# Mamba and mixture-of-experts block on one core: row sums by accumulating DMA, f16 dt projection, a folded prologue, a new instruction order, and the residual added by TensorE

## The reference

```python
h = layernorm(x) * (1 + ca) + sa
x = x + ga * mamba(h)          # mamba(h) = out_proj(y) + h
h = layernorm(x) * (1 + cb) + sb
x = x + gb * moe(h)

# mamba: xi, z = split(rmsnorm(h) @ in_proj); xi = silu(causal conv of 4 taps (xi))
#   dt (16), B (16), C (16) = split(xi @ x_proj);  delta = softplus(dt @ dt_proj + b)
#   state (512 channels x 16): s = s * exp(delta * A) + delta * B * xi, along the sequence
#   y = (sum over the 16 states of s * C) + xi * D;  y = y * silu(z)
# moe: 16 experts and a shared one (two more in the kernel's layout); sigmoid gate, the 4 largest
#   of 16 normed as weights; silu(x @ win) * (x @ vin) * weight, @ wout, summed
```

## Time and profile before

| | |
|---|---|
| time, median of 3 runs | 3053.87 us (3050.2 to 3055.23) |
| profiled execution | 3054.61 us, span of its records 3052.8 us |
| TensorE matmuls busy | 2488.1 us (82%), 16524 instructions |
| VectorE busy | 2568.1 us (84%), 3986 |
| ScalarE busy | 1830.3 us (60%), 3484 |
| GpSimd busy | 2563.1 us (84%), 2379 |
| DMA | 187.97 MB, mean 62 GB/s |

### The profile page before, as it was taken

The page is one execution under the profiler, slowest core; times in us unless marked ns, Lnnn a source line. Parts: engine busy times, 40 slices in busy tenths (PEclk is TensorE's granted clock), DMA queues, the critical chain, the costliest instruction groups (busy, mean ns, idle before and its releaser), DMA issues.

```text
span 3052.8 us, 52878 instructions
## 1 busy us (share of the span) xinstructions
PE 2488.1 (82%) x16524; PEld 1983.2 (65%) x16524; DVE 2568.1 (84%) x3986; ACT 1830.3 (60%) x3484; POOL 2563.1 (84%) x2379
## 2 busy tenths in 40 slices
PE   2566988879888797988879798887979888797979
PEld 0344766757676675767667576776757667576767
DVE  3579899888898988889898888889888898988953
ACT  2666666666666665665657566665656656665531
POOL 1689898989989898998989889898988989898942
PEclk7557998999999998999989899999989999999989
DMA  1311111211112111121112111121212211111101
GB/s 64 107 56 58 64 56 64 71 57 61 56 61 72 62 61 53 60 68 64 63 52 77 56 60 59 64 66 55 74 41 73 68 56 60 60 58 58 67 32 49
DMA packets 62150, 187.97 MB, mean 62 GB/s; under 512 B 12040, under 2 KB 14728, under 8 KB 61488
## 3 DMA queue, kind: packets, MB, share of 16 engines
q1 hardware_dynamic: 61872, 184.58, 18.0%
HBM read 166.68 MB, written 17.87 MB: 60 GB/s over the span
## 4 chain that ended last, share of the span: by engine, by line
POOL 29%; PE 27%; DVE 17%; issue 16%; ACT 9%; DVEq 1%; POOLq 1%; ACTq 0%; DMA 0%
POOL db_sb L639 12%; PE bank_ps L1236 9%; DVE states L995 7%; POOL y_sb L651 6%; PE moe_ps L1251 6%; PE rows_ps L1178 5%; POOL act L681 3%; POOL y_sb L659 2%; PE bank_ps L1160 2%; ACT da_ps L839 2%; DVE y_sb L1014 2%; DVE bank_ps L950 2%; DVE act L1089 1%; PE bank_ps L1134 1%; POOL du_sb L628 1%
## 5 line engine op out<-in xcount | busy, mean ns | idle before, releaser
L639 POOL TENSOR_TENSOR db_sb<-du_sb,b_sb 128x512 f32<-128x512 f32 x1024 | 1296.6, 1275 | 0.1
L1178 PE MATMUL rows_ps<-ident,states 128*128 128x128 f32 x4096 | 673.2, 295 | 163.7 <-DVE states L995 94.3
L651 POOL TENSOR_TENSOR y_sb<-y_sb,c_rows 128x512 f32<-128x512 f32 x512 | 655.1, 1280 | 169.8 <-ACT c_rows L817 169.8
L839 ACT ACTIVATE da_ps<-delta,a_sb 128x512 f32<-128x512 f32 x1024 | 701.8, 687 | 85.7 <-DVE states L995 84.2
L1178 PEld LDWEIGHTS rows_ps<-ident,states 128*128 128x128 f32 x4096 | 535.3, 153 | 281.9 <-DVE states L995 133.0
L1251 PE MATMUL moe_ps<-eout_sb,act 128*128 128x256 f32 x2304 | 627.7, 396 | 85.2 <-POOL act L681 83.5
L1236 PE MATMUL bank_ps<-h2T_high,ein_w_high 128*128 128x256 f16 x2304 | 644.0, 280 | 21.8 <-DVE delta L971 12.0
L995 DVE TENSOR_TENSOR_SCAN states<-da_ps,carry,db_sb 128x512 f32<-128x512 f32 x512 | 648.4, 1274 | 15.0 <-ACT da_ps L839 13.2
L1236 PE MATMUL bank_ps<-h2T_high,ein_w_low 128*128 128x256 f16 x2304 | 643.1, 279 | 0.0
L1236 PE MATMUL bank_ps<-h2T_low,ein_w_high 128*128 128x256 f16 x2304 | 642.4, 279 | 0.0
L995 DVE TENSOR_TENSOR_SCAN states<-da_ps,db_sb 128x512 f32<-128x512 f32 x512 | 616.2, 1213 | 23.2 <-ACT da_ps L839 13.0
(11 more groups left out here) (156 smaller groups left out, 2851.1 us busy)
## 6 DMA issues: line engine op xcount, KB each, us to landing
b_sb<-b_dram SPq DMA_DIRECT2D x128, 512.0 KB, 3.6
w_sb<-w_dram SPq DMA_DIRECT2D x128, 512.0 KB, 4.0
th_p<-x_dram SPq DMA_DIRECT2D x16, 512.0 KB, 5.8
r_dram<-conv SPq DMA_DIRECT2D x16, 512.0 KB, 2.6
x<-r_dram SPq DMA_DIRECT2D x16, 512.0 KB, 3.8
out_dram<-x SPq DMA_DIRECT2D x32, 256.0 KB, 2.2
mod_p<-mod_dram SPq DMA_DIRECT2D x8, 384.0 KB, 6.2
x<-e_in_dram SPq DMA_DIRECT2D x5, 512.0 KB, 4.6
```

The source lines that it names most:

```text
L639: pool.tensor_tensor(db_sb[:, n % NDB, :], du_sb[:, slots[t][0][0], b, :], b_sb[:, k % NBPAIR, s % BPAIR, :], ALU.mult).then_inc(sem["scal ...
L651: pool.tensor_tensor(place, place, c_rows[:, n % NCR, :], ALU.add).then_inc(sem["c_added"], 1)
L839: ac.activation(da_ps[n % NDA][:, :], delta[:, slots[t][0][0], b, :], ACT.Exp, scale=a_sb[:, b, s:s + 1]).then_inc(sem["exp_done"], 1)
L1178: last = pe.transpose(rows_ps[j % 2][:, b * P:b * P + P], states[:, step % 2 * NB + b, j * P:j * P + P], ident[:, :])
```

## The change

* **Rows.** ScalarE scales all four row blocks (`c_scale`), two at a time into one buffer of `c_rows`. `gather` is gone, and `c_add` is no GpSimd addition but a DMA that GpSimd issues for each pair of row blocks and that adds 128 x 1024 numbers into `y_sb`; the next step's DMA of the same pair waits for its landing.
* **Residual.** `r_gate`, `r_add`, `r_store` are gone. h itself is stored (`h_store`) and loaded again in the mix stage (`h_load`, into a new buffer `h_mix`); TensorE adds it in the out projection's bank, by a matmul with the identity, and `r_load` fetches x. The gate row leaves `mod_p`.
* **dt.** `xd` is computed transposed, four f32 matmuls of 512 columns that give 48 rows. ScalarE (`dt_high`) and VectorE (`dt_low`) split dt into f16 halves stacked on 80 partitions (`dt16`), against weights stacked likewise, so that `dtp` is four f16 matmuls. `xd_evac` is now ScalarE's and makes the rows directly; four transposes give C back as columns (`xd_t_evac`, VectorE).
* **Buffers.** `NDB` 6 to 5, `WROWS` 4 to 1: one expert's weights for each load, two buffers of one.
* **Prologue.** The blocks before slot 0 are gone. Their steps stand in the common order before and within slot 0 and wait only for what they need; x is the fourth load; the first sequence's modulation rows are computed first, with the condition vector repeated in 128 columns, and copied from PSUM (`mod0_rows`). No semaphores are cleared.
* **Order.** All places in the order are set anew: constants, `SHIFT` by name, and new tables `PLACE` (by name and index), `FIRST`, `LAST` and `START`.

```diff
-NDA, NDB, NCR = 2, 6, 3
-C_ACT = (1, 3)
-C_DVE = tuple(j for j in range(NJ) if j not in C_ACT)
+NDA, NDB, NCR = 2, 5, 3
+CPAIR = 2
...
-WROWS, NWROWS = 4, 2
+WROWS, NWROWS = 1, 2
...
-LEAD_P0, LEAD_P, LEAD_M = 2.059, 8.0, 1.42
...
-SLOT = 67.197
...
+LEAD_P0, LEAD_P, LEAD_M = 6.1001, 7.9891, 2.1125
...
+SLOT = 70.6876
...
+                    def first_loads():
+                        sp.dma_start(ct_sb, c_t).then_inc(sem["ct_in"], 16)
+                        sp.dma_start(wmod_sb[:, :, 0:2 * DM], w_mod[:, :, 0:2 * DM]).then_inc(sem["wmod_in0"], 16)
+                        sp.dma_start(norm_sb[:, :], norm_w).then_inc(sem["in_w_in"], 16)
+                        x_load(0)
+                        sp.dma_start(in_raw, in_w).then_inc(sem["in_w_in"], 16)
...
-                    def r_store(t):
-                        sp.wait_ge(sem["r_made"], nP(t) + 1)
...
+                    def h_store(t):
+                        for half in range(2):
+                            sp.wait_ge(*h_done(t, half))
+                        sp.dma_start(h_dram[bass.ds(slots[t][1][1], 1)].rearrange("o p n -> (o p) n"),
+                                     h_sb.rearrange("p j n -> p (j n)")).then_inc(sem["h_out"], 16)
...
+                    def h_load(t):
+
+                        sp.wait_ge(sem["h_out"], 16 * nP(t - 1))
+                        if nM(t):
+                            sp.wait_ge(*bank_full(("op", last_mix(t), NJ - 1)))
...
-                    def c_add(t, s, j):
+                    def c_add(t, s, pair):
...
+                        if step:
+                            pool.wait_ge(*c_adds(n - NJ // CPAIR))
...
-                        pool.tensor_tensor(place, place, c_rows[:, n % NCR, :], ALU.add).then_inc(sem["c_added"], 1)
+                        pool.dma_start(y_sb[:, slots[t][0][0], CPAIR * pair:CPAIR * pair + CPAIR, :], c_rows[:, n % NCR, :, :],
+                                       accum_op=ALU.add).then_inc(c_adds(n)[0], 16)
...
                         ac.wait_ge(sem["h_rms_done"], nP(t) + 1)
-                        ac.wait_ge(sem["r_gated"], nP(t) + 1)
+                        ac.wait_ge(sem["h_out"], 16 * (nP(t) + 1))
...
+                        for at in (DT_HIGH, DT_AGAIN):
+                            ac.activation(dt16[at:at + RANK, :], bank(("xd", t))[0:RANK, :], ACT.Copy).then_inc(sem["dt_high_done"], 1)
...
+                        ac.activation(c_rows[:, n % NCR, j % CPAIR, :], rows_ps[j % 2][:, :], ACT.Copy,
+                                      scale=xd_sb[:, slots[t][0][0], j, s:s + 1]).then_inc(sem["c_scaled"], 1)
...
-                        for j in range(NJ):
-                            for b in range(NB):
-                                last = pe.matmul(bank(key)[:, j * XD:j * XD + XD], u_sb[:, b, j * P:j * P + P], xproj_sb[:, b, :],
-                                                 start=(b == 0), stop=(b == NB - 1))
+                        for b in range(NB):
+                            last = pe.matmul(bank(key)[0:XD, :], xproj_sb[:, b, :], u_sb[:, b, :], start=(b == 0), stop=(b == NB - 1))
...
-                        pe.matmul(bank(key), dtw_sb[:, b * P:b * P + P], xdT[0:RANK, :], start=True, stop=True).then_inc(bank_full(key)[0], 1)
+                        pe.matmul(bank(key), dtw16[:, b * P:b * P + P], dt16[:, :], start=True, stop=True).then_inc(bank_full(key)[0], 1)
...
-                            pe.wait_ge(*(c_scales(*before) if before[1] in C_ACT else gathers(*before)))
+                            pe.wait_ge(*c_scales(*before))
...
                         for b in range(NB):
-                            last = pe.matmul(bank(key)[:, 0:DM], yT[:, j % 2, b, :], out_sb[:, b, :], start=(b == 0), stop=(b == NB - 1))
+                            pe.matmul(bank(key)[:, 0:DM], yT[:, j % 2, b, :], out_sb[:, b, :], start=(b == 0), stop=False)
+                        pe.wait_ge(sem["h_in"], 16 * (nM(t) + 1))
+                        last = pe.matmul(bank(key)[:, 0:DM], ident[:, :], h_mix[:, j, :], start=False, stop=True)
```

More of the change, by code:

```diff
@@ L88, in prepare_steps @@
     out += [(8 + 0.3 * j, ("h_square", t, j)) for j in range(NJ)]
-    out += [(10, ("h_rms", t)), (10.5, ("r_gate", t)), (11.5, ("r_add", t)), (11.6, ("r_store", t))]
+    out += [(10, ("h_rms", t)), (7.9, ("h_store", t))]
     for j in range(NJ):
@@ L110, in mix_steps @@
 def mix_steps(t):
-    out = [(-0.9, ("r_load", t))]
+    out = [(-0.9, ("r_load", t)), (-0.9, ("h_load", t))]
     for j in range(NJ):
@@ L155, in schedule @@
-def schedule(slots, load_mod_p, load_mod_m, first_block):
+LEAD_P0, LEAD_P, LEAD_M = 6.1001, 7.9891, 2.1125
+TICK, ROUTED, UNITS_END = 1.4758, 16.0, 63.872
+SOFT = 45.5812
+Z_AHEAD, Y_SOON, Y_LATE = 0.2928, 0.2445, -0.1899
+SLOT = 70.6876
+SHIFT = {"b_load": -2.314, "b_store": 0.735, "c_add": 0.79, "c_scale": 0.59, "carry": -0.619, "ct_silu": -0.08, "ct_tanh": -0.183,
+         "delta": -0.11, "dt_bias": -0.033, "dt_low": 0.821, "dtp": 0.038, "du": -0.32, "e_act": -0.086, "e_mul": -0.086, "e_tanh": -0.337,
+         "e_weigh": 0.709, "ein_high": 0.74, "ein_load": 1.067, "ein_low": -1.703, "eout_fold": 2.072, "eout_load": -0.127, "exp": 0.887,
+         "expert_in": -0.107, "expert_out": 0.74, "fold": 1.006, "gather": 0.59, "h2_high": 0.438, "h2_low": 1.268, "h2_scale": 0.228,
+         "h2_t": 0.443, "h_rms": -0.354, "h_scale": -0.55, "h_square": -0.36, "hn_high": -0.86, "hn_low": -0.55, "hn_t": -0.58,
+         "in_low": -0.545, "logit": 1.048, "logit_exp": 0.32, "mod0_rows": 0.371, "mod_m_load": 0.05, "mod_rows": 2.349, "mods": 0.216,
+         "op": 0.52, "op_gate": 0.507, "out_add": -0.126, "out_gate": -0.197, "out_store": 0.393, "r_add": 3.787, "r_gate": -0.15,
+         "r_store": 0.1, "router": 1.898, "rows": 0.29, "scaled": -0.083, "scan": -0.15, "skip": -1.623, "skip_evac": -0.34,
+         "skip_t": -0.302, "soft_exp": -0.848, "soft_ln": 0.933, "tap": -0.024, "u": -0.714, "u_tanh": -0.714, "w_evac": 1.163,
+         "w_load": -0.107, "w_store": -1.614, "w_t": 1.126, "x1": 0.523, "x1_norm": 0.703, "x1_rstd": -0.248, "x1_stat": 0.52,
+         "x_load": -2.297, "x_norm": 0.671, "x_rstd": -0.656, "x_scale": 0.42, "x_stat": 0.151, "xd": 0.045, "xd_evac": 0.152,
+         "xd_t": 0.072, "xd_t_evac": 0.855, "xi": 0.112, "xi_center": 0.256, "xi_copy": 0.112, "y_evac": 0.386, "y_gate": -0.101,
+         "y_t": 0.622, "z": -0.763, "z_gate": -0.93, "z_tanh": -0.773}
@@ new lines, with place, start_steps @@
+START = {"constants": 0.018, "ct_tanh": -1.588, "first_loads": 5.582, "fold": 1.987, "in_high": -3.563, "in_low": 0.718, "mod0": 0.251,
+         "mod_rows": -0.032, "mod_store": -0.045, "mods": 1.704, "out_scale": -2.535}
+def place(what):
+    return "_".join(str(n) for n in (what[0], *(what[3:] if what[0] in ("exp", "scaled", "scan", "rows", "c_scale", "c_add") else what[2:])))
+def start_steps():
+    out = [(-9, ("first_loads",)), (-9, ("constants",)), (-8, ("ct_tanh",)), (-8, ("ct_silu",)), (-7, ("mod0",)), (6.2, ("mod0_rows",))]
+    out += [(-6, ("norm_lift",))] + [(6.3, ("in_high", k)) for k in range(NK)] + [(7.6 + 3.0 * k, ("in_low", k)) for k in range(NK)]
+    out += [(7.7, ("fold",)), (10.7, ("mods",)), (18.5, ("mod_rows",)), (18.5, ("mod_store",)), (18.5, ("a_made",)), (12.0, ("out_scale",))]
+    return out
@@ L172, in schedule @@
             steps += [(at - LEAD_M if t == 0 else at, what) for at, what in mix_steps(t)]
-        out += [(SLOT * t + at + SHIFT.get(what[0], 0.0), t, n, what) for n, (at, what) in enumerate(steps)]
+        ends = FIRST if t == 0 else LAST if t == len(slots) - 1 else {}
+        for n, (at, what) in enumerate(steps):
+            at = round(at + SLOT * t + SHIFT.get(what[0], 0.0) + PLACE.get(place(what), 0.0) + ends.get(what[0], 0.0), 5)
+            latest[what[0]] = max(at, latest.get(what[0], at))
+            out.append((latest[what[0]], t, n, what))
     order = [what for _, _, _, what in sorted(out, key=lambda x: (x[0], x[1], x[2]))]
@@ L272, in adaln_block @@
         x1 = sb("x1", [P, NJ, DM])
+        h_mix = sb("h_mix", [P, NJ, DM])
         h2 = zg[:, :, :].rearrange("p a (b n) -> p (a b) n", n=DM)
```

433 lines of the change are left out of this document (239 added, 194 removed), and 52 rows, old and new, of the table PLACE.

## The result

The changed kernel takes 3128.02 us, median of 4 runs (3112.68 to 3134.75), against 3052.82 (3050.2 to 3055.23) for the kernel before on the same chip: ratio 1.0239, 95% interval 1.0201 to 1.0278. It is slower by 2.4%; I had forecast 2825 us. The profiled execution is the shortest of the four, 3112.68 us (span 3110.9); what follows adds up to it, and the median lies 15 us higher.

A forecast was written before the change was run, and what follows sets the result against it. GpSimd's load plus waits of a tight interleaving was taken as the bound, VectorE and TensorE close behind. 3054.6 - 32 (prologue) - 8 (slot 1) - 187 (slots 2 to 15) - 6 (slot 16) + 3 (tail) = 2824.6; range 2690 to 3000.

The forecast's parts named there:

- The prologue: Work before the first scan product: x loaded fourth, product at about 76 us instead of 108, together 32 us less.
- The tail: Units after the last scan: single-row loads beside TensorE's 2.18 us a unit or just over; 3 us charged with last landing.
- The busy sums: Forecast busy us per steady slot: GpSimd 149.4, TensorE 152.0, ScalarE 136.6, VectorE 135.5.
- The issue's price: GpSimd's cost to issue one accumulating DMA: 1.1 us taken, bounds 0.43 and 2.37, 32 issues a slot.
- the two-pass case: DMA engines: an accumulation costs two plain passes, 3.1 us, so 134 of a 166 us slot, hidden.
- Order and buffers: Single-row weight loads in two buffers: hidden by about 10 us of lead; 1 us a slot charged, from 0 to 5.
- the accumulate's check: Whether accumulations fit the sixteen DMA engines: two passes give 134 of 166 us, three give 184, over the slot.
- The gap: Slot time above GpSimd's busy time: 19.8 us before, 16.6 kept, giving a slot of 166.
- B: Rival: late single-row loads, ScalarE alone between scan and both row banks; slot 174, 2945 us; chance 0.20.
- A: Rival: GpSimd's accumulating issue nearly free, about 0.5 us, TensorE the bound; slot 155, 2660 us; chance 0.16.
- C: Rival: each accumulating issue costs GpSimd 2 us; GpSimd 178, slot 184; chance 0.14 shared with D.
- D: Rival: three-pass accumulations fill DMA engines, `c_add` waits for landings; slot 184 or more, 3095 us; chance 0.14 shared with C.

## Why the forecast failed

**What held.** The prologue: 77.47 us against "about 76". The tail: last scan product at 2973.3 to the end is 137.6 us, against 135.3 before, +2.3 for the 3 charged. The busy sums: GpSimd 144.6 (149.4), TensorE 153.8 (152.0), ScalarE 132.3 (136.6), VectorE 139.3 (135.5). The issue's price, the term with the widest bounds: 0.95 us as load by the subtraction above, 0.90 to 0.91 by the runs with fewer issues and 1.05 of the slot for each added one, for the 1.1 taken, with an issue now counted as busy, against what I had said. TensorE's parts: `xd` 3.6 us a slot for 4.5, `dtp` 1.5 for 1.7, the identity product 28.6/12 = 2.4 for 2.0. A term that was off without deciding anything is the store of h: it lands after 6.5 us in the median, not 2.6, so that "equal" is wrong for the wait of `h_scale`; store, load and product together cost 1.97 us a slot by the run without them.

**The accumulate.** All its DMA time is 0.460 x 3110.9/512 = 2.80 us of the sixteen engines for each, against 3.1 assumed and 1.56 for a plain pass worked out in the prediction. DMA share of the slots 0.70 for "near 80%". That is near the two-pass case that the Trainium skill gives ("Collectives: The Full Stack", on the bandwidth ceiling), and the trace agrees in size: 1.8 plain passes. The time to landing is another matter: 5.5 us in the median. By the Trainium skill, "DMA: Bandwidth & Descriptors", the anatomy of a DMA issued from GpSimd, the estimates are 3.2 us for 512 KB and 2.3 for 128 KB. The traces lie above both, with 5.5 us, and 3.3 for 128 KB at quarter size on less loaded engines.

**The step that failed** is in *Order and buffers*: "it is hidden unless two weightings come in a row. I charge 0 to 5 us a slot and take 1, inside the gap below." It cost 10 us a slot (four early buffers return 10.3; two loads a chunk 11.6). The sign was to be "few GpSimd waits on `w_sb`", and they are 209.0 us. Two things in that step were wrong. I took the flight from the kernel before as bounded by 4.0 us, which is a median (the longest of its loads took 5.8), though the change lifts the DMA share from 0.18 to 0.70: it became 3.6 in the median and 9.0 at the longest. And I took 10 us, twice a thirty-sixth of the slot, as the lead. But the 36 units stand between places 12 and 64 of the slot's 67: with single rows in the kernel before, only 7.1 us pass in the mean from the weighting that frees a buffer to the one that needs it. Of these the load loses what it stands on SyncE behind `b_load`, which itself waits for GpSimd, 2.9 us in the median where it does. The step knew that the scan's products stand behind `e_weigh` and still charged 1 us.

**The second part of it** is under the accumulate's check: 134 of 166 us of DMA time, "hidden". A busy share under one hides nothing that somebody waits for. Beyond what the row buffers can cure, quarter-size accumulations return 3.4 us a slot (174.11 to 170.66), nearly all of it (3.1) GpSimd's wait for the step before's accumulation to land.

**The gap.** With both cured the slot is 170.7, 4.7 over the forecast's 166, and GpSimd's busy time still 144.8: the gap above it is 25.8 us, not "I keep 16.6". In that run GpSimd waits for VectorE's states (75.0 us in twelve slots) and activations (65.2) and for ScalarE's rows (56.3); in the kernel before the first was not among its waits, the second 41.1 and the third 129.7. VectorE in turn waits for ScalarE's activations (126.3, before 57.5) and for its `exp` (80.6, before 13.1). So the chain runs back to ScalarE, which has 132 us of work a slot where it had 113; whether its load or the new order makes these waits was not tried, and stays open.

**In us of the span.** From 166 to 184.4 are 18.4 a slot: 13.7 from rows and DMA load together, 4.7 from the gap. Over 14 slots that is 257 us, of the 288 between 2824.6 and 3112.7. The rest shows when the span is cut at GpSimd's first scan product of each slot: slot 1 lasts 152.8 us where the kernel before has 147.9, slot 16 159.8 for 153.0, slots 2 to 15 together 75.0 more than before. Against -8, -6 and -187 in the sum these are 13, 13 and 262 us. Slot 16 is the late rows: with four early buffers it lasts 146.2 us, where the sum had 147. Slot 1 has no row loads, and its DMA share is 0.80: four early buffers leave it at 153.5, and with quarter-size accumulations besides it lasts 145.6.

**Luck and sums.** The range was said to hold with 0.8, but its parts as given, 0.50 for the forecast, 0.20 for B and a fifth of A's 0.16, make 0.73. That the four busy sums came within 5 us of the trace is no luck: each term but the issue's price came from a row. The price itself, 1.1 between 0.43 and 2.37, was a choice that came out.

**The rivals.** A (issue nearly free) fell with the 0.95 us. C (2 us) too. B had the place right, single rows late, at a slot of 174; it left out the load on the flights, and so its price was 10 us short. Its other half, ScalarE between the scan and both banks, does not show where B put it: GpSimd's wait for ScalarE's rows fell from 129.7 to 56.8 us. D named the side on which the time fell and the DMA load as its origin, but its mechanism did not set this time: an accumulation takes 2.80 us of the engines, not over 4.6, and `c_add` waited 21.3 us in the whole run for accumulations to land. It appears once the rows are in time, with 54.6 us in twelve slots. It took B's order and D's load at once: single rows in the old order without accumulations (ratio 0.9995) are no slower than before, and the accumulations with rows in time (0.9663) are faster. That I had given them as alternatives, each with its own chance, is why the case of both had none.
